# Weights of ten stages loaded by SyncE in the stage before, one stage's loads issued by two engines, and a changed number of unread products on TensorE

## The reference

```python
x = _layernorm(x + _L0_attn_ref(x, ...))          # 16 heads of 32, gate, positions; own layer norm behind
x = _layernorm(x + _L0_xattn_ref(x, ctx, ...))    # 8 heads of 128
x = _layernorm(x + _L0_ffn_ref(x, ...))           # 32 experts, 4 for each row, and a shared one
x = _layernorm(x + _L1_attn_ref(x, ...))          # 16 query heads of 64, 4 key heads, rotary positions
x = _layernorm(x + _L1_xattn_ref(x, ctx, ...))    # 16 heads of 16, biases
x = _layernorm(x + _L1_ffn_ref(x, ...))           # 8 experts, 2 for each row
x = _layernorm(x + _L2_attn_ref(x, ...))          # one head of 256
x = _layernorm(x + _L2_xattn_ref(x, ctx, ...))    # 4 heads of 64
x = _layernorm(x + _L2_ffn_ref(x, ...))           # distances to 32 prototypes, rank-16 products
x = _layernorm(x + _L3_attn_ref(x, ...))          # 16 heads of 16 over a latent of 256 -> 128
x = _layernorm(x + _L3_xattn_ref(x, ctx, ...))    # 16 heads of 64, layer norms in front
x = _layernorm(x + _L3_ffn_ref(x, ...))           # 8 experts, exact gelu
```

```python
attn = jnp.einsum('bqhd,bkhd->bhqk', q, k) * scale        # causal: -inf above the diagonal
out  = jnp.einsum('bhqk,bkhd->bqhd', softmax(attn), v)    # then the output weights
```

## Time and profile before

| | |
|---|---|
| median of three runs | 3228.99 us (3226.81 to 3235.66) |
| the profiled execution: its own time, its span | 3227.85 us, 3226.0 us |
| PE busy | 2640.8 us, 82% of the span |
| DVE busy | 1856.3 us, 58% |
| ACT busy | 1478.4 us, 46% |
| POOL busy | 995.8 us, 31% |
| granted TensorE clock, mean | 0.923 |
| unread products (L4679) | 893, busy 237.0 us |

### The profile page before, as it was taken

The page is one execution under the profiler, slowest core; times in us unless marked ns, Lnnn a source line. Parts: engine busy times, 40 slices in busy tenths (PEclk is TensorE's granted clock), DMA queues, the critical chain, the costliest instruction groups (busy, mean ns, idle before and its releaser), DMA issues. The chain is left out here.

```text
span 3226.0 us, 46804 instructions
## 1 busy us (share of the span) xinstructions
PE 2640.8 (82%) x16783; PEld 1448.3 (45%) x16783; DVE 1856.3 (58%) x5014; ACT 1478.4 (46%) x2984; POOL 995.8 (31%) x822
## 2 busy tenths in 40 slices
PE   6888887896678678888886689998888799979987
PEld 2323334564444323333353265565444233346666
DVE  6576664566655555555553558235431677655678
ACT  5334452464432256666641524214412355537876
POOL 1145562146347566666622300001101111101200
PEclk9889998998889879999997889999899799989999
DMA  3221101520454411111002210001001322014023
GB/s 112 84 54 42 43 3 36 196 85 24 121 160 99 109 51 46 31 46 46 17 15 65 37 40 1 10 4 31 15 1 41 67 32 38 3 48 124 1 79 105
DMA packets 186949, 174.63 MB, mean 54 GB/s; under 512 B 52777, under 2 KB 160042, under 8 KB 186462
## 3 DMA queue, kind: packets, MB, share of 16 engines
q1 hardware_dynamic: 172030, 153.84, 17.0%
q0 software_dynamic: 9408, 12.56, 2.5%
q10 hardware_dynamic: 5280, 5.24, 0.5%
HBM read 117.62 MB, written 57.40 MB: 54 GB/s over the span
## 5 line engine op out<-in xcount | busy, mean ns | idle before, releaser
L953 POOL TENSOR_TENSOR l1a_p_lo<-res,l1a_p_hi 128x1024 f16<-128x1024 f32 x192 | 311.6, 1641 | 173.1 <-ACT res L1198 173.1
L4679 PE MATMUL ps<-ident_b 128*128 128x512 bf16 x893 | 237.0, 413 | 56.1 <-PEq L111 26.7
L1207 ACT ACTIVATE l0a_probs<-ps 128x1024 f32<-128x1024 f32 (+1 forms) x192 | 145.4, 810 | 175.4 <-PE ps L1061 103.1
L1207 ACT ACTIVATE l3a_probs<-ps 128x1024 f32<-128x1024 f32 (+1 forms) x192 | 146.1, 808 | 146.8 <-PE ps L1061 119.5
L1197 ACT ACTIVATE l1a_p_hi<-ps 128x1024 f16<-128x1024 f32 x192 | 158.0, 823 | 109.8 <-PE ps L1061 82.8
L1058 PE MATMUL ps<-l1a_qs,l1a_ks 128*128 128x512 f16 (+3 forms) x768 | 166.1, 331 | 31.4 <-ACT res L1198 31.4
L1023 PE MATMUL ps<-l1a_ks,l1a_qs 128*128 128x512 f16 (+3 forms) x384 | 121.3, 345 | 78.0 <-DVE l1a_nmax L1232 33.0
L1229 DVE CUSTOM_DVE_ANT_0 l1a_masked<-ps,l1a_wide_mask 128x128 bf16<-128x128 f32 (+3 forms) x256 | 118.0, 489 | 103.0 <-PE ps L1023 100.7
L4679 PEld LDWEIGHTS ps<-ident_b 128*128 128x128 bf16 x893 | 88.2, 104 | 180.9 <-issue 75.5
L978 POOL TENSOR_TENSOR l0a_both<-l0a_probs 128x768 f32<-128x768 f32 (+2 forms) x96 | 154.5, 1631 | 46.3 <-PE ps L1099 46.1
L1198 ACT ACTIVATE res<-ps 128x1024 f32<-128x1024 f32 x192 | 158.5, 825 | 0.0
(11 more groups left out here) (751 smaller groups left out, 6507.3 us busy)
## 6 DMA issues: line engine op xcount, KB each, us to landing
f_wf<-in_L_ffn_w_dram SPq DMA_DIRECT2D x16, 1024.0 KB, 6.7
f_slots<-x0a_zeros SPq DMA_DIRECT2D x32, 256.0 KB, 3.4
f_xe<-f_slots SPq DMA_DIRECT2D x32, 256.0 KB, 3.1
f_ys<-f_y SPq DMA_DIRECT2D x32, 256.0 KB
l1a_qs<-l_q_h SPq DMA_DIRECT2D x64, 128.0 KB
d_wall<-in_L_ffn_W_dram SPq DMA_DIRECT2D x3, 2112.0 KB
l0a_qs<-l_q_h SPq DMA_DIRECT2D x32, 128.0 KB
l0a_ks<-l_k_h SPq DMA_DIRECT2D x16, 256.0 KB
```

What stands on the lines that cost most here:

```text
L953: pool.tensor_tensor(ph_lo[:, n % SLOTS, :, 0:w], probs[:, n % FULL, :, 0:w], ph_hi[:, n % SLOTS, :, 0:w], ALU.subtract).then_inc(s_["low_ ...
L1207: act.activation(probs[0:KR, n % SLOTS, 2 * pr:2 * pr + 2, 0:w], SB[x % 2][:, :, 0:w], ACT.Exp).then_inc(s_["exps"], 1)
L4679: pe.matmul(bank, self.ident_b[:], self.ident_b[:, None, :].to_broadcast([P, 4, P]), start=True, stop=True)
```

## The change

**Ahead.** A new class `Ahead` holds tiles that outlive a stage, a semaphore and a list of loads. SP issues the loads with `issue` in the stage in front, and the engines of the stage itself only `wait`. So are loaded: the output weights of `l0o` (in `l0a`) and of `x1o` (in `x1a`), the context and key weights of `x0c` (in `l0o`), `x2c` (in `l2o`) and `x3c` (in `l3o`), the query weights and bias of `x1p` (in `x1c`), the weights of `l2p` (in `f1`), the prototypes of `f2` (in `x2a`), the weights of `l3e` (in `f2`) and of `l3p` (in `l3e`). In each the loads stand behind the front stage's own loads on SP; in `l0a` they stand in front of the last three rounds of small DMAs.

**Two issuers.** In `x1c` the eight loads are issued by SP and ACT in turn instead of by SP alone.

**Unread products.** They are dropped at the starts of `l0o`, `x1o`, `x0c`, `x2c`, `l2p`, `l3e`, `l3p`, `x1p`, in `l0p` (0, 4, 4 and 9 a batch), in `x3c` (nine before each of four transpositions), in `l3a` (nine a step) and in `f2` (four a tile). In `x2a` there are four instead of two a tile. Those of `Tail`, of `x1c` and at the start of `f2` stay.

```diff
+class Ahead:
+    def issue(self, sp):
+        for dst, src in self.loads:
+            sp.dma_start(dst, src).then_inc(self.sem, 16)
+    def wait(self, eng):
+        eng.wait_ge(self.sem, 16 * len(self.loads))
...
@@ norm_program (x3c)
+            pe.wait_ge(ph.s["n_xc_ready"], g + 1)
             if g >= NB:
                 pe.wait_ge(ph.s["n_ready"], g - NB + 1)
-            if within:
-                k.keep_busy(pe, TP[g % NB][:, 0, :], 9)
-            pe.wait_ge(ph.s["n_xc_ready"], g + 1)
@@ packed_attention, SP behind the steps' loop
+                if following:
+                    following.issue(sp)
                 for s in range(S - LEAD - 1, S) if split or paired else ():
@@ packed_attention, PE (l3a)
                         pe.wait_ge(s_["maxed"], a - NSA + 1)
-                        if own_sums and plan.key_rows == P:
-                            k.keep_busy(pe, sa, 9)
                         pe.wait_ge(r_ld[s % KEEP], 32 * (s // KEEP + 1))
@@ project_columns (l0o, x1o)
-                k.keep_busy(pe, k.ps[:, 2, :], 16 if pre else 12)
-                pe.wait_ge(ph.s["w_ld"], n_ld)
+                given.wait(pe)
@@ l0p
-                            if b:
-                                pe.wait_ge(ph.s["v_ready"], b * TB)
-                            k.keep_busy(pe, PV[0], (0, 4, 4, 9)[c])
@@ project_in (l2p, l3p, x1p)
-            k.keep_busy(pe, k.ps[:, 0, :], busy)
-            if not apart:
-                pe.wait_ge(ph.s["w_ld"], 16 * len(loads))
+            given.wait(pe)
@@ l3e
-                    k.keep_busy(pe, k.ps[:, 0, :], 14)
-                    pe.wait_ge(ph.s["w_ld"], 80)
+                    given.wait(pe)
@@ context (x1c)
-                for dst, src in loads:
+                for dst, src in loads[0::2]:
                     sp.dma_start(dst, src).then_inc(ph.s["ld"], 16)
+                if following:
+                    following.issue(sp)
...
+                for dst, src in loads[1::2]:
+                    act.dma_start(dst, src).then_inc(ph.s["ld"], 16)
@@ cross_operators (x0c, x2c)
-                    k.keep_busy(pe, bank[0], 16 if shared else 11)
@@ cross_rows (x2a)
-                        k.keep_busy(pe, TP[x % 2], 2)
+                        k.keep_busy(pe, TP[x % 2], 4)
@@ f2
+                    pe.wait_ge(s_["weighted"], t + 1)
                     if t >= 2:
                         pe.wait_ge(s_["moved"], t - 1)
-                        k.keep_busy(pe, TP[t % 2], 4)
-                    pe.wait_ge(s_["weighted"], t + 1)
```

More of the change, by code:

```diff
@@ L1283, in _, with project_columns @@
                     item(a)
-def project_columns(k, name, o_t, FC, wo, x_in, bias=None, pre=None):
+def project_columns(k, name, o_t, FC, x_in, given, following=None):
     nc = k.nc
     with Phase(k, name) as ph:
[L1294 to L1299, removed]
+        w, pre = given.w, given.own
+        tail = Tail(ph, x_in, given.bias, pre)
+        ph.sems.append(given.sem)
         Y = [k.ps[:, b:b + 2, :].rearrange("p b (t d) -> p (b t) d", d=D) for b in (2, 6)]
@@ L1306, in _ @@
             def _(sp):
[L1307 to L1314, removed]
+                for g in range(NG):
                     tail.load(sp, g)
+                if following:
+                    following.issue(sp)
             @block.tensor
             def _(pe):
-                k.keep_busy(pe, k.ps[:, 2, :], 16 if pre else 12)
-                pe.wait_ge(ph.s["w_ld"], n_ld)
+                given.wait(pe)
                 for g in range(NG):
@@ L1844, in row_parts, with project_in @@
     return parts
-def project_in(k, ph, jobs, loads, split=False, early=None, apart=False, busy=8):
+def project_in(k, ph, jobs, split=False, early=None, given=None, by_batch=False):
     nc = k.nc
@@ L1869, in _ @@
         def _(sp):
-            for (dst, src), sem in zip(loads, w_ld):
-                sp.dma_start(dst, src).then_inc(sem, 16)
             for b in range(B):
@@ L1910, in _ @@
         def _(act):
-            if not apart:
-                act.wait_ge(ph.s["w_ld"], 16 * len(loads))
             for b in range(B):
@@ L2567, in cross_attention @@
                     for c in range(FC)]
-            project_in(k, ph, jobs, loads, split=stack is not None, early=early if stack else None)
+            project_in(k, ph, jobs, split=stack is not None, early=early if stack else None, given=given)
+        given.ctx.close()
         if stack:
-            packed_attention(k, f"{name}a", plan, G, stack, qt, kt, v_all, o_t, first=early)
-            project_columns(k, f"{name}o", o_t, FV // P, wo, None, bias=bo)
+            given = ahead_of_columns(k, f"{name}o", FV // P, wo, bias=bo)
+            packed_attention(k, f"{name}a", plan, G, stack, qt, kt, v_all, o_t, first=early, following=given)
+            project_columns(k, f"{name}o", o_t, FV // P, None, given)
+            given.ctx.close()
         else:
@@ L2642, in turned_context @@
                 pe.wait_ge(ph.s["cleared"], 3)
-                pe.wait_ge(ph.s["k_ld"], 16 * len(first))
+                given.wait(pe)
                 if norm is not None:
@@ L2719, in context_rows @@
                 if norm is not None:
-                    dve.wait_ge(ph.s["k_ld"], 16 * len(first))
+                    given.wait(dve)
                     for b in range(B):
@@ L2773, in _ @@
             def _(sp):
-                for dst, src in first:
-                    sp.dma_start(dst, src).then_inc(ph.s["k_ld"], 16)
                 for dst, src in second:
@@ L3639, in l1_feed_forward @@
     TERMS = [(0, 0), (0, 1), (1, 0)]
+    following = k.ahead["l2p"] = Ahead(k, "l2p")
+    following.w = following.sb("w", [P, DC, 3 * D])
+    following.loads = [(following.w[:, :, i * D:(i + 1) * D], weight_rows(a[f"L2_attn_{m}"])) for i, m in enumerate(("Wq", "Wk", "Wv"))]
     with Phase(k, "f1") as ph:
```

171 lines of the change are left out of this document (110 added, 61 removed).

## The result

| | before | after |
|---|---|---|
| median of 13 runs | 3230.76 us | 3214.35 us |
| ratio, 95% interval | | 0.9949 (0.9934 to 0.9964) |
| profiled execution: span | 3226.0 us | 3213.6 us |
| unread products | 893 | 560 |

The account below looks back on a forecast made before the run. TensorE, busy 82% of the span, was taken to bound most stages, though 237.0 us were unread products. Early loads 25.2 us plus unread products 14.1 gave 39.3 us, so 3189 us, range 3172 to 3215.

Parts of the forecast that it names:

- the starts: Stage starts: real products begin sooner after the barrier with early loads; 25.2 us in all after 1.0 for contention.
- the six rows of the table: Predicted gains: l0o 4.1, x0c 4.3, x1c with x1p 6.0, x1o 3.0, l2p 2.8, l3e with l3p 6.0 us.
- l3a: Stage l3a, bounded by TensorE: dropping nine unread products a step gains 17.0 less 3.4 for the clock, 13.6 us (5 to 17).
- I take two falls here, each costing 1.7 us: Even steps of l3a: TensorE's standstill drops the clock twice, taking 3.4 us from the stage's gain.
- the 1.4: Even steps of l3a, where the wait for r_row takes the dropped products' place: 1.4 us gained for all.
- rival A: Whole kernel: the clock takes most of the gain back, in l3a, x3c, l0p, f2 and the starts; 3217 us, chance 0.17.
- x3c and l0p: Dropping unread products inside these stages gains 2.5 us in x3c (-2 to 4.5) and 3.0 in l0p (0.5 to 4.2).
- f2: Stage f2: dropping four unread products a tile makes the clock fall more often, net loss 2.5 us (-8 to +2.5).
- rival D: Front stages' SP queues end in a wait, so loads are issued only at their end; 3214 us, chance 0.02.
- contention: Loads of l0o and x1o run beside small DMAs of the attention in front: cost 1.0 us in all (0 to 4).
- x2c: Start of x2c: early load gains nothing, since TensorE would only wait for DVE instead of the DMA.
- x2a: Stage x2a: two more unread products a tile cost 4.8 us, clock kept gives 2.3 back, net loss 2.5 (-6.5 to +2).

## Why the prediction was wrong

**Right: the starts.** The method of the first real product less the exit from the barrier gave 26.2 us for the six rows of the table; 25.5 came, against one profile of the kernel before. Against the profile with only l3a changed the same stages are 23 us shorter (x0c 2.0 instead of 4.8), so single rows are good to 2 or 3 us. The two issuers of x1c and the single loads were not tried one by one.

**Wrong: l3a, the step that failed.** I had counted which groups are late and which are free: eight late, eight covered by the wait for r_row. That count was right but for step 14, so the late ones gave 13.4 us instead of 15.6. The step that failed is the next: "I take two falls here, each costing 1.7 us". Six waits of eight brought a fall, five of them new, and the low time behind the first 34 us of l3a went from 1 to 27 us. Dropping the eight covered groups lost 8.6 us, where I had 3.4 lost for the clock less 1.4 gained: the 1.4 did not come, since all of the groups' time became standstill, and the products took 8.2 us longer. A fall cost about what I had said (8.2 us for five new ones and a longer low stretch in step 15); their number was wrong. With the kernel that kept these eight groups it is shown that they were what held the clock up. I had leaned on l1a's thirteen waits of 2.32 us, with one fall. Those waits are shorter than the 2.4 to 3.8 us that arose here, and I had this length in hand: 0.63 us and 1.9 us is 2.5, already longer, before a late landing is added. This is rival A's mechanism in its first item (8.5 us more for l3a), while its other items didn't come: x3c and l0p did better than I had, f2 cost only 1. That 3214 is also the time of rival D is chance: D has the loads not early at all, and the starts refute it.

What of l3a's gain of 4.8 us reached the kernel may be less still: l3a alone gave a ratio of 0.9999, with some 6 us of room either way. l3o behind it took 29.8 to 30.7 us in the four profiles with none of l3a's groups, and 27.4 and 27.9 in the two with all sixteen. With eight groups, that of step 15 among them, it was 28 us three times and 31 three times, so the end of l3a isn't its only cause.

**Wrong by size: contention.** I had 1.0 us in all (bounds 0 and 4), and x1a alone lost 2.6 to 3.8. The place was the one I named, the tail of small DMAs; I had not added that a wait of 3.6 us also costs clock, nor that it is the small DMA issued behind the load that is late.

**Wrong: x2c.** "Nothing" was right for the wait and wrong for the clock: +4.2 us. I had argued that TensorE would only wait for DVE instead of the DMA, and had not asked what TensorE does in that wait.

**Wrong by size: x2a.** Two more products a tile cost 4.4 us between the two profiles, and 8.2 us against the kernel with the early loads alone. I had 4.8 for the products and gave 2.3 back for clock they would hold. They hold none beyond what two hold.

**The sum.** Of the 39.3 us, l3a lacks 8.8, x2c 4.2, x1a 1.6, x2a 1.9; l0p and x3c gave 2.2 more, f2 1.5 more, x1c and the like 0.7 less. That leaves 25.8. (From the median the forecast would have been 3189.7; I wrote 3189.) The measured 16 us are 9 us less than that. Part of it lies in how one execution differs from another (l1a alone covers 9 us): the one profile of the kernel before that all these differences rest on is itself 2.9 us under its median of thirteen, and short in the stages that the change doesn't touch. In x0a, whose code didn't change, all eleven profiles of kernels with early loads lie above the two without (200.6 to 202.9 us against 198.9 and 199.4). Why was not tried; it stays open, and so does the rest of the 9 us.

## What to carry to other kernels

An unread product that stands in a wait costs nothing and may be what holds the clock; one that stands where nothing is awaited costs its full time. Sort them place by place and drop only the second kind: here that was worth more than dropping all. When an edit turns busy time into standstill, price the clock behind it as well as the wait, by waits of the same length in the same kind of stage. And an early load is issued where the front stage has no small, urgent DMAs: the same load at the start of x1a cost nothing that shows, and at its end 2.6 to 3.8 us, as much as the 2.8 us that it won.

## What the hardware showed that I had not expected

A small DMA of 4 KB issued 0.34 us behind a load of 512 KB, from another engine, landed after 4.5 us instead of 2.2, while one issued 0.34 us ahead of that load landed after 2.2 as ever. Standstills of 2.4 to 3.8 us brought the clock down in five of six cases in l3a, in each of four profiles, and those of 0.6 to 1.9 us in one of seven. And one kernel's median differed by 10 us between two chips, while its six runs on each lay within 9 us (3191.6 to 3198.7 against 3201.1 to 3209.9) and the kernel before showed no such difference.
